# Loops written out in an attention and slot network kernel, with token sums taken pairwise and the normalisation moved to GpSimd

## The reference, cut to what matters

```
h = gelu(concat(xn, slot_mean) @ w1 + b1)            # xn: x, normalised per token
logits = (h @ w2 + b2) / (abs(tau) + 0.1)            # 64 slots
alpha = softmax of the 8 largest logits, 0 elsewhere
slot_input = einsum('bts,btd->bsd', alpha, xn)       # the token sums
si = slot_input / alpha.sum(over the tokens)
# then, small: a GRU, attention among the 64 slots of a batch, a layer norm, projections
out = einsum('bts,bsd->btd', alpha, slot_values)     # x + 0.5 * out
```

## Time and profile before

| what | value |
|---|---|
| profiled execution, its own time | 3877.5 us |
| its span, first to last instruction | 3875.7 us |
| median of three runs | 3881.76 us |
| PE busy | 3571.8 us, 92% |
| DVE busy | 3064.9 us, 79% |
| ACT busy | 2771.7 us, 72% |
| Pool busy | 745.2 us, 19% |
| mean granted TensorE clock | 0.969 |

### The profile page before, as it was taken

One profiled execution on the slowest core, in us unless ns is written; L12 is line 12 of the kernel. 1 busy time (PEld: TensorE's weight loads), 2 busy tenths in 40 slices (PEclk: granted clock), 3 DMA queues, 4 the chain that ended last, 5 costly groups with the idle time before them and its releaser, 6 DMA issues. The chain is left out here.

```text
span 3875.7 us, 74183 instructions
## 1 busy us (share of the span) xinstructions
PE 3571.8 (92%) x22026; PEld 1297.7 (33%) x22026; DVE 3064.9 (79%) x4493; ACT 2771.7 (72%) x5460; POOL 745.2 (19%) x835
## 2 busy tenths in 40 slices
PE   7997599999999999999999999999999999967997
PEld 4653223323232323232323233232323232214653
DVE  6965688888888888888888888888888888826865
ACT  5730188888887878887878787878787878875730
POOL 2310211212121212121212112121212121102310
PEclk8999699999999999999999999999999999998999
DMA  3226202121212111111111111111111111112226
GB/s 108 87 78 283 59 19 56 30 63 31 66 39 53 40 51 50 42 51 45 47 48 48 45 49 43 51 41 51 41 51 41 51 40 51 29 43 87 87 78 282
DMA packets 123164, 247.44 MB, mean 64 GB/s; under 512 B 34656, under 2 KB 75424, under 8 KB 108464
## 3 DMA queue, kind: packets, MB, share of 16 engines
q1 hardware_dynamic: 115712, 208.06, 19.1%
q10 hardware_dynamic: 7088, 34.61, 2.2%
HBM read 121.91 MB, written 51.38 MB: 45 GB/s over the span
## 5 line engine op out<-in xcount | busy, mean ns | idle before, releaser
L1331 DVE TENSOR_REDUCE attn_part_max<-attn_ps 128x2 f32<-128x1024 f32 x2048 | 2455.1, 1222 | 473.2 <-PE attn_ps L1456 466.8
L1568 ACT ACTIVATE attn_probs<-attn_ps 128x512 f32<-128x512 f32 x4096 | 2182.1, 599 | 426.0 <-PE attn_ps L1468 425.5
L1468 PE MATMUL attn_ps<-attn_q_rows,attn_k_rows 50*128 50x512 f16 x4096 | 1271.9, 386 | 68.6 <-ACT attn_probs L1568 59.3
L1456 PE MATMUL attn_ps<-attn_k_rows,attn_q_rows 48*128 48x512 f16 x4096 | 1151.7, 391 | 78.8 <-issue 37.6
L1482 PE MATMUL attn_ps<-attn_probs,attn_v_ones 128*32 128x512 f32 x8192 | 1104.0, 611 | 0.7 <-ACT attn_probs L1568 0.7
L1468 PEld LDWEIGHTS attn_ps<-attn_q_rows,attn_k_rows 50*128 50x128 f16 x4096 | 277.6, 94 | 1327.6 <-ACT attn_probs L1568 1248.8
L1456 PEld LDWEIGHTS attn_ps<-attn_k_rows,attn_q_rows 48*128 48x128 f16 x4096 | 224.1, 94 | 197.9 <-DVE attn_part_max L1331 131.4
L1411 PE MATMUL attn_ps<-attn_xn_t,attn_w_qk 128*128 128x256 f32 x1024 | 289.0, 406 | 0.7 <-ACT attn_xn_t L1513 0.7
L1482 PEld LDWEIGHTS attn_ps<-attn_probs,attn_v_ones 128*32 128x32 f32 x8192 | 161.9, 108 | 339.8 <-issue 293.8
L1220 POOL TENSOR_TENSOR attn_pool_waited<-ones 128x1 f32<-128x1 f32 x144 | 27.8, 193 | 1270.8 <-ACT attn_max_whole L1551 655.4
L1261 POOL TENSOR_TENSOR attn_ctx_t<-attn_o_packed,attn_inv_wide 128x1024 f32<-128x1024 f32 x32 | 75.4, 2358 | 932.0 <-DMA attn_inv_wide<-inverse_denominators 610.4
(11 more groups left out here) (161 smaller groups left out, 2450.2 us busy)
## 6 DMA issues: line engine op xcount, KB each, us to landing
attn_q_rows<-attn_parts SPq DMA_DIRECT2D x384, 64.0 KB, 2.2
attn_k_rows<-attn_parts SPq DMA_DIRECT2D x384, 64.0 KB, 2.2
ffn_x_ring<-in_L_attn_x SPq DMA_DIRECT2D x16, 1024.0 KB, 5.8
attn_x_ln<-after_first_ffn SPq DMA_DIRECT2D x16, 1024.0 KB, 4.9
attn_o_packed<-attn_o_sb SPq DMA_DIRECT2D x256, 64.0 KB, 2.3
attn_inv_wide<-inverse_denominators SPq DMA_DIRECT2D x32, 512.0 KB
attn_x_res<-after_first_ffn SPq DMA_DIRECT2D x16, 1024.0 KB, 4.8
after_attention<-attn_x_res SPq DMA_DIRECT2D x16, 1024.0 KB, 8.4
```

What stands on the lines that cost most here:

```text
L1331: dve.tensor_reduce(part_max[:, G % 2, :, j, t, half], pair, AX.X, ALU.max).then_inc(dve_emptied, 1)
L1456: last = pe.matmul(ps[:, bank + e, :], q_rows[rows_e, G % NG, j, t * P:(t + 1) * P], k_rows[rows_e, G % NG, j, half * HALF:(half + 1) * HA ...
L1468: pe.matmul(ps[:, bank, :], k_rows[rows_e, G % NG, h // 2, kt * P:(kt + 1) * P], q_rows[rows_e, G % NG, h // 2, half * HALF:(half + 1) * H ...
L1568: act.activation(probs[:, quad % NQ, h, :], bank_of(s, b0), ACT.Exp, scale=1.0 / (SCALE * SCALE)).then_inc(act_emptied, 1)
```

## The change

Every `Fori` loop is replaced by written-out code (`for b in range(B)`), in both FFN parts and in the attention. In the FFN's front part, further: the token sums of a pair of batches are made together, tile by tile, batch 2p into partitions 0 to 63 and batch 2p+1 into 64 to 127, half of the tiles in step 2p+3 and half in step 2p+4. Pool normalises all eight tiles of x (L332 in the new file), in place of four on DVE and four on ACT, and the small product `shift` is gone. `statistics` runs two steps ahead in place of one, with two buffers of its results. The ring of x has eight buffers in place of four. `divide` moves from odd to even steps, `turn_sums` from even to odd ones.

```
-    R = 4
+    R = 8
...
-            def over_batches(eng, step):
-                for b in range(R):
-                    step(b, 0, b, b)
-                with eng.Fori(1, B // R - 1, 1) as q:
-                    for r in range(R):
-                        step(q * R + r, q, r, R + r)
-                for b in range(B - R, B + 3):
-                    step(b, b // R, b % R, b)
+            STEPS = B + 5
...
             @block.sync
             def _(sp):
+                for b in range(B):
+                    if b >= R:
+                        sp.wait_ge(si_ready, (b - R) // 2 + 1)
+                    sp.dma_start(x_ring[:, b % R, :, 0:D], rows(x_in, b)).then_inc(x_loaded[b % R], 16)
...
             def _(pool):
+                def normalise(b):
+                    pool.wait_ge(rstd_ready, b + 1)
+                    for low, made in ((0, xn_low), (LOW, xn_high)):
+                        for t in range(low, low + LOW):
+                            last = pool.tensor_scalar(x_ring[:, b % R, t, 0:D], x_ring[:, b % R, t, 0:D], mean_var[:, b % 2, t, 0:1],
+                                                      rstd[:, t:t + 1], ALU.subtract, ALU.mult)
+                        last.then_inc(made, 1)
...
+                for n in range(B + 1):
                     if n + 1 < B:
+                        rsqrt(n + 1)
+                    if n >= 1:
+                        less_largest(n - 1)
+                    if n + 1 < B:
+                        normalise(n + 1)
+                    if n >= 1:
+                        scale(n - 1)
...
             def _(dve):
-                def normalise(b, r):
-                    dve.wait_ge(rstd_ready, b + 1)
-                    dve.scalar_tensor_tensor(shift[:, :], mean_var[:, :, 0], -1.0, rstd[:, :], ALU.mult,
-                                             ALU.mult).then_inc(shift_set, 1)
-                    for t in range(LOW):
-                        last = dve.tensor_scalar(x_ring[:, r, t, 0:D], x_ring[:, r, t, 0:D], mean_var[:, t, 0:1],
-                                                 rstd[:, t:t + 1], ALU.subtract, ALU.mult)
-                    last.then_inc(xn_low, 1)
...
+                for n in range(STEPS):
                     if 1 <= n <= B:
+                        find_top(n - 1)
+                    if n + 2 < B:
+                        statistics(n + 2)
                     if 1 <= n <= B:
+                        weigh(n - 1)
+                    if n % 2 == 0 and 4 <= n <= B + 2:
+                        divide((n - 4) // 2)
...
             def _(pe):
+                def sum_tokens(pair, tiles):
                     if tiles[0] == 0:
+                        pe.wait_ge(alpha_ready, 2 * pair + 2)
+                        if pair >= 1:
                             pe.wait_ge(si_taken, pair)
                     for t in tiles:
+                        for e in range(2):
+                            last = pe.matmul(ps_si[e * S:(e + 1) * S, 0:D + 1], alpha[:, pair % 2, t, e, :], x_ring[:, (2 * pair + e) % R, t, :],
+                                             start=(t == 0), stop=(t == TT - 1), skip_group_check=True)
...
+                    if n < B:
+                        turn_rows(n, (0, 1))
+                    if summing:
+                        sum_tokens(pair, (first,))
                     if n < B:
+                        turn_rows(n, (2, 3))
+                    if summing:
+                        sum_tokens(pair, (first + 1,))
+                    if n % 2 and 5 <= n <= B + 3:
+                        turn_sums((n - 5) // 2)
                     if n < B:
+                        hidden(n)
+                    if summing:
+                        sum_tokens(pair, (first + 2, first + 3))
+                    if n % 2 and summing:
+                        turn_weights(pair)
                     if n < B:
+                        logits(n)
...
-            body(0, 0)
-            with eng.Fori(1, B - 1, 1) as b:
-                body({1: b, "eng": eng, **{rate: eng.snap(b * rate) for rate in rates}}, B0)
-            body(B - 1, B - 1)
+            for b in range(B):
+                body(b, b)
```

More of the change, by code:

```diff
@@ L261, in build_ffn @@
             rstd = sb("rstd", [P, TT], F32, own)
-            shift = sb("shift", [P, TT], F32, own)
             xn_t = sb("xn_t", [P, KT, T], F32, own)
@@ L516, in _ @@
                 pe.wait_ge(ones_set, 1)
-                def step(b, q, r, n):
-                    def sums(*tiles):
-                        if 2 <= n <= B + 1:
-                            sum_tokens(b - 2, q * (R // 2) + (r - 2) // 2, (r - 2) % R, n - 2, tiles)
+                for n in range(STEPS):
+                    pair, first = (n - 3) // 2, 0 if n % 2 else TT // 2
+                    summing = 0 <= pair < PAIRS
                     if n < B:
-                        turn_rows(b, r, n, (0, 1))
-                    sums(0)
+                        turn_rows(n, (0, 1))
+                    if summing:
+                        sum_tokens(pair, (first,))
@@ L526, in step @@
                     if n < B:
-                        turn_rows(b, r, n, (2, 3))
-                    sums(1, 2, 3)
-                    if n < B:
-                        hidden(b, n)
-                    if n % 2 == 0 and n >= 4:
-                        turn_sums(pairs_of(q, r))
-                    sums(4, 5, 6, 7)
-                    if n % 2 and 3 <= n <= B + 1:
-                        turn_weights(pairs_of(q, r), r, n)
+                        turn_rows(n, (2, 3))
+                    if summing:
+                        sum_tokens(pair, (first + 1,))
@@ L541, in _ @@
             def _(act):
-                def normalise(b, r):
-                    act.wait_ge(shift_set, b + 1)
-                    for t in range(LOW, TT):
-                        last = act.activation(x_ring[:, r, t, 0:D], x_ring[:, r, t, 0:D], ACT.Identity,
-                                              bias=shift[:, t:t + 1], scale=rstd[:, t:t + 1])
-                    last.then_inc(xn_high, 1)
-                normalise(0, 0)
-                def step(b, q, r, n):
-                    flat = xn_t[:, :, :].rearrange("p k t -> p (k t)")
+                flat = xn_t[:, :, :].rearrange("p k t -> p (k t)")
@@ L574, in step @@
+                        act.wait_ge(at_ready, pair + 1)
+                        act.activation(alpha_t[:, pair, :].rearrange("p (n h) -> p n h", h=HALF),
                                        ps_at[:, :, :], ACT.Identity).then_inc(at_taken, 1)
-                    if n % 2 == 0 and n >= 4:
-                        act.wait_ge(si_turned, pairs - 1)
-                        act.activation(si_t[:, :, bass.ds((pairs - 2) * P, P)],
-                                       ps_at[:, 0, 0:D].rearrange("p (k s) -> p k s", k=KT),
-                                       ACT.Identity).then_inc(si_t_ready, 1)
@@ L580, in _ @@
-                over_batches(act, step)
         RP = 4
@@ L887, in over_pairs @@
             def over_pairs(eng, step):
-                step(0, True)
-                with eng.Fori(1, PAIRS // RP, 1) as q:
-                    step(q, False)
+                for q in range(PAIRS // RP):
+                    step(q, q == 0)
             @block.sync
```

136 lines of the change are left out of this document (58 added, 78 removed).

## The result

The changed kernel takes 3866.25 us (median of 17 runs) against 3891.85 of the kernel before on the same chips, a ratio of 0.9956 with a 95% interval of 0.9937 to 0.9975. That is 0.4% faster. The forecast was 3769 us, some 3% faster. The range missed it too.

A forecast was written before the change was run, and what follows sets the result against it. PE was taken to set the steady FFN step, DVE close behind. Saving 57.7 us in the attention and 52.6 in the FFNs, 110.3 together, gave 3767.2 from the profiled execution, 3771.5 on the median; forecast 3769, range 3740 to 3805.

The forecast's parts named there:

- Part 3, Pool's tile: FFN front part: Pool's eight normalise tiles take 0.553 us each, 8.4 us of load in 10.6, costing nothing.
- Pool becomes the bound: FFN step: tiles take 1.1 us beside DVE if ports are shared, Pool has 12.8 us, time 3841; chance 0.08.
- level: FFN's end: last pair's sums with turn_weights between, 1.9 + 1.0 + 1.9 for 3.9 + 1.0, no change.
- Part 1, the attention: Attention loop: thirteen jumps back at 4.44 us each disappear in written-out code, 57.7 us.
- the waits with registers cost nothing visible: Attention loop: waits with registers taken as zero beyond the jump back.
- The jump's own 4.44: Attention loop: each jump back costs 4.44 us, 2.9 idle and some 1.5 at the low clock.
- Part 2, the sums: FFN token sums on PE: two halves run side by side, making 3.87 us per step into 1.94.
- The step: FFN front part: the chain through ACT sets even steps at 10.2 us and odd ones at 11.0, mean 10.6.
- The start: Each FFN's start: eight tiles on Pool where four ran on each of two engines, 1.8 us later.
- The exclusion of VectorE and Pool: FFN step: mutual blocking taken as zero; as a rival, 17.5 us per step and 3980, chance 0.02.
- The rival of instruction supply: Attention: written-out code has the jump's stall too, elsewhere, so only the FFN part is gained, 3829; chance 0.06.

The follow-up runs named there:

- pool_add: The changed kernel with Pool adding a negated mean in the FFN's normalise where it subtracted the mean: 3767.34 us, ratio 0.9682.
- attn_two: The kernel before with two bodies per round of its attention loop (7 rounds for 14): 3861.35 us in one run.
- the probes: The changed kernel with an added block before the first FFN, where Pool does eight tiles in each of several forms; no kernel time given.

## Why the prediction was wrong

**Part 3, Pool's tile, is the step that failed.** I priced L332 by the attention's L1251: "Pool gains eight of 0.553, 4.42 us, and has 1.84, 1.08 and again some 1.08: 8.4 us in 10.6." Shape, type and instruction agree; the operations don't (SUBTRACT for ADD), and that stood in the diff. It measured 1.24 us. Pool then has 9.9 + 3.7 = 13.6 us, and the steady step is that; where I had 1 to 2.5 us to spare there is nothing, and PE's transposes wait for Pool. The rival "Pool becomes the bound, 12.8 us, 3841" had the mechanism, by ports, at a chance of 0.08; its cause was another. The row for `attn_neg_mean` should have raised the question why that kernel takes the trouble to negate a mean.

**With that one price mended, the sum comes out, in part by luck.** The kernel with the add form takes 3764 to 3767, for a forecast of 3769. Between the profiled executions of before and of pool_add lie 119.1 us, where the forecast had 110.3: the attention gives 70.5 for 57.7 and the steps 61.0 for 56.2, while the two starts cost 8.6 for 3.6, and the stretches behind step 16 another 3.8 that the forecast put at nothing ("level"). These errors cancel in part. The parts:
- Part 1, the attention: 57.7 forecast, 69.3 measured (13 x 5.33). Mis-sized term: "the waits with registers cost nothing visible". Counts in registers cost 0.92 us per body. I had compared a body with the loop's first round, which waits on registers too; 184.50 in attn_two is the 184.47 that I read there. The jump's own 4.44 was right for the kernel before.
- Part 2, the sums: the mechanism was right. Halves run side by side, 2.4 us by the rows' durations for my 1.94; from start to start, as I had counted the 3.87, it is 0.58 + 0.59 + 1.02, 2.2 us (odd step of pool_add).
- The step: 10.2 and 11.0 forecast, 10.13 and 10.71 measured in pool_add.
- The start: +1.8 forecast; +9.5 and +10.5 in the changed kernel with the dear tiles, +2.1 to +5.5 with the cheap ones. I had no term for the first hidden at the low clock.
- The exclusion of VectorE and Pool: taken as zero, which was near enough: a tile takes 568 ns in the mean in pool_add and 554 to 565 in the probes with VectorE idle, and the dear tiles' 1.24 us are 1.22 to 1.23 there.
- The rival of instruction supply: wrong. PE's "issue" waits of the earlier trace rows are gone, and no others came.
- The statistics' lead of two steps I gave no term of its own. With the order of Pool's rsqrt, it carries about 70 us once Pool does the normalise.

**The slow end of the attention** in the profiled execution, 20.2 us, is no part of the forecast's error, which is about 100 us in the medians. What lets the clock fall there in some executions stays open: PE is busy for 53.4 of the 58.5 us while it is low, and I changed nothing that would tell it.

## What to carry to other kernels

A price from another place of the trace holds for the same operations, not only for the same instruction, shape and engine: compare the operands' names and the code's line, and where a kernel goes out of its way (a mean that is negated first), ask what it avoids. When a helper engine is to take over work, put its whole load per step beside the step, and see at which price it becomes the bound; here that was 0.84 us a tile ((10.4 - 3.7) / 8), between the price that I took and the one that came. To price a loop's jump, compare with written-out code and not with the loop's own first round.

## What the runs showed of the hardware

- Pool's scalar-pointer instruction on f32, 128x256: 0.55 to 0.57 us for add then multiply or multiply then add; 1.22 for subtract or max then multiply, multiply then subtract, subtract then add; 0.92 for a single add or subtract. The Trainium skill, page "GPSIMD Engine Reference", section "Engine selection", calls Pool roughly line-rate with one input. If the cheap pair's 0.84 ns per column is that rate, which no run here shows, it does not hold for subtract then multiply, at 3.3.
- Pool's eight cheap tiles: 4.31 us beside BN_STATS, 7.20 beside six two-input VectorE adds in SBUF (3.7 us of them by themselves), 5.60 beside six one-input ones (2.1 us).
- A jump back cost 4.1 us in the mean in attn_two and 4.4 in the kernel before, and counts in registers 0.9 us per body of 184. The Trainium skill, page "Runtime: NRT & Kernel Launch", section "Instruction fetch mechanics", says that a taken branch to code outside the fetched window stalls; the idle time without a releaser agrees, and no run here shows the fetch itself.
- Two column halves that take turns matmul by matmul run side by side: a step's eight sums take 2.4 us. With all eight in one half they take 4.1 us, and the step is 1.27 us longer.
- PE's first hidden of an FFN took 5.6 to 6.6 us for 3.70, at the low clock for part of it (0.50 to 0.52 in pool_add), in 16 of 18 starts where Pool made the first tiles, and in 2 of 10 where VectorE and ACT did (6.0 and 5.4).
